# Scan of a Mamba block: the C product of five state indices on ScalarE in turned form, eight B products on GpSimd

## The reference

```python
x = silu(conv1d_depthwise(x, conv_w, 4 taps) + conv_b)           # 512 channels, 2048 steps
dt, Bm, Cm = split(x_proj_w @ x, [16, 32])                       # rank 16; 16 rows of B; 16 rows of C
dt = softplus(dt_w @ dt + dt_b)
A = -exp(A_log)                                                  # 512 x 16
def step(h, inp):
    h = exp(dt_t[..., None] * A) * h + (dt_t * u_t)[..., None] * B_t[:, None, :]
    return h, einsum('bdn,bn->bd', h, C_t)
y = ys + D * x
return y * silu(z)
```

## Time and profile before

| | |
|---|---|
| runs (us) | 8468.7, 8469.42, 8474.6; median 8469.42 |
| profiled execution | span 8471.3; no time beside the span is listed for it |
| scan phase in it | about 2600 to 6040 us after the span's start |
| busy over the span | TensorE 7608.0 (90%), VectorE 7340.3 (87%), ScalarE 5072.8 (60%), GpSimd 3704.5 (44%) |
| scans, L2022 | 2048, 1684.6 + 771.8 us busy |
| C products by GpSimd, L1707 | 1024, 2412.4 us busy |
| granted clock of TensorE, mean | 0.954 |

### The profile page before, as it was taken

One profiled execution on the slowest core, in us unless ns is written; L12 is line 12 of the kernel. 1 busy time (PEld: TensorE's weight loads), 2 busy tenths in 40 slices (PEclk: granted clock), 3 DMA queues, 4 the chain that ended last, 5 costly groups with the idle time before them and its releaser, 6 DMA issues. The chain is left out here.

```text
span 8471.3 us, 131822 instructions
## 1 busy us (share of the span) xinstructions
PE 7608.0 (90%) x38817; PEld 3068.7 (36%) x38818; DVE 7340.3 (87%) x10750; ACT 5072.8 (60%) x7665; POOL 3704.5 (44%) x1825
## 2 busy tenths in 40 slices
PE   6999999989987888888888888888889999999899
PEld 3333333325542333333333333333453333333355
DVE  6988888858877999999999999999658888888588
ACT  3577777762255666666665556556316777777622
POOL 0010011100016999999999999999400000110000
PEclk9899999989998999999999999999988999999999
DMA  6001101112262222222233333333561001010121
GB/s 177 18 19 20 19 19 19 20 37 70 67 232 91 85 83 83 84 83 83 83 98 103 100 100 100 101 103 97 164 181 18 19 19 19 19 22 18 36 78 61
DMA packets 531283, 603.88 MB, mean 71 GB/s; under 512 B 195488, under 2 KB 344736, under 8 KB 526560
## 3 DMA queue, kind: packets, MB, share of 16 engines
q1 hardware_dynamic: 526048, 562.63, 22.4%
q0 software_dynamic: 4608, 33.56, 2.0%
HBM read 397.75 MB, written 163.69 MB: 66 GB/s over the span
## 5 line engine op out<-in xcount | busy, mean ns | idle before, releaser
L833 DVE TENSOR_REDUCE ffn_att_mx<-psum 128x1 f32<-128x512 f32 (+3 forms) x4608 | 2728.0, 654 | 367.8 <-PE psum L674 209.2
L794 ACT ACTIVATE ffn_att_e<-psum,unscale 128x1024 f32<-128x1024 f32 (+3 forms) x2560 | 2376.5, 985 | 766.3 <-PE psum L739 760.3
L1707 POOL TENSOR_TENSOR scan_h<-scan_h,scan_cs 128x1024 f32<-128x1024 f32 x1024 | 2412.4, 2449 | 203.8 <-ACT scan_state L1878 198.0
L1788 PE MATMUL psum<-scan_h,ident 128*128 128x512 f32 x4096 | 1977.7, 624 | 158.9 <-POOL scan_h L1707 157.6
L2022 DVE TENSOR_TENSOR_SCAN scan_h<-psum,scan_state,scan_db 128x512 f32<-128x512 f32 x1408 | 1684.6, 1261 | 10.5 <-ACT psum L1920 10.5
L641 POOL TENSOR_SCALAR_AFFINE_SELECT ffn_att_e<-ffn_att_e 128x512 f32<-128x512 f32 x512 | 324.6, 634 | 3023.9 <-ACT ffn_att_e L794 3023.9
L674 PE MATMUL psum<-ffn_att_k,ffn_att_q 48*128 48x512 f16 (+3 forms) x5120 | 1438.8, 367 | 175.4 <-DMA ffn_att_v<-v 55.8
L1788 PEld LDWEIGHTS psum<-scan_h,ident 128*128 128x128 f32 x4096 | 777.7, 198 | 1321.1 <-issue 894.5
L705 PE MATMUL psum<-ffn_att_e,ffn_att_v 128*32 128x512 f32 (+3 forms) x10240 | 1240.4, 557 | 7.8 <-ACT ffn_att_o L809 2.4
L1920 ACT ACTIVATE psum<-scan_dt,scan_anr 128x512 f32<-128x512 f32 x1024 | 698.2, 682 | 460.2 <-DVE scan_h L2022 459.4
L674 PEld LDWEIGHTS psum<-ffn_att_k,ffn_att_q 48*128 48x128 f16 x5120 | 394.8, 94 | 1559.4 <-DVE ffn_att_mx L833 1260.7
(11 more groups left out here) (256 smaller groups left out, 7118.0 us busy)
## 6 DMA issues: line engine op xcount, KB each, us to landing
scan_cs<-scan_bcd SPq DMA_DIRECT2D x520, 256.0 KB, 3.2
scan_bs<-scan_bcd SPq DMA_DIRECT2D x162, 256.0 KB, 3.4
scan_win<-xp SPq DMA_DIRECT2D x34, 1036.0 KB, 7.0
scan_dt<-scan_sp POOLq DMA_DIRECT2D x32, 1024.0 KB, 7.0
mamba_out_ffn_in_ys<-yz SPq DMA_DIRECT2D x18, 1024.0 KB, 7.6
scan_yi<-y SPq DMA_DIRECT2D x17, 1024.0 KB, 6.7
ffn_att_q<-q_parts SPq DMA_DIRECT2D x128, 128.0 KB, 2.8
ao<-ffn_att_on SPq DMA_DIRECT2D x128, 128.0 KB
```

The lines of the kernel that those rows point to most:

```text
L794: nc.scalar.activation(E[:, s % PB, 2 * hp:2 * hp + 2, off:CH], psum[:, 2 * hp:2 * hp + 2, off:CH], ACT.Exp, scale=unscale[:, 0:1]).then_i ...
L833: nc.vector.reduce_max(mx[:, hh * 2 + pairs[0]:hh * 2 + pairs[1], i // HALF, i % HALF, c // TT], psum[:, turn, 0:(pairs[1] - pairs[0]) * w ...
L1707: nc.gpsimd.tensor_tensor(hh, hh, cs[:, n % NCS, :].unsqueeze(1).to_broadcast([P, 2, CH]), ALU.mult).then_inc(hc_ready, 1)
L1788: ins = nc.tensor.matmul(psum[:, m, :], ident[:, :], h[n % NH][:, m, :], start=False, stop=n == DS - 1)
```

## The change

Indices 5, 7, 9, 11, 13 (`TURN_N`) get another way to their C product. TensorE transposes h block by block (128 steps of all four tiles at a time, `turn_state`) into `BANK_X`, so that steps lie on partitions. There C_n is one number per partition: ScalarE's `times_c` copies the bank to SBUF with it as scale. TensorE transposes that back, adding into the sum (`turn_back`). C itself is turned once a chunk (`turn_c`, `keep_c`). The other eleven indices (`ROW_N`) keep GpSimd's product, now one instruction over four tiles, with one state copy for all four tiles. `POOL_N` grows from five to eight; `dbp` has two buffers and `db` one. TensorE sums an index two slots after its scan (`LAG`); `skip` and `read_y` move from slot 1 to 2; the convolution of a tile is one piece in slots 7, 9, 11, 13, and its copy follows in slots 8, 10, 12, 14. `dt_proj` of tiles 2 and 3 stands behind sums of its slot, and softplus_in comes in slots 3, 4, 4 and 5.

```diff
-    NH, NCS = 4, 8
-    POOL_N = (3, 6, 9, 12, 15)
+    NH, NT = 4, 4
+    TURN_N = (5, 7, 9, 11, 13)
+    ROW_N = [n for n in range(DS) if n not in TURN_N]
+    POOL_N = (1, 4, 6, 8, 10, 12, 14, 15)
+    POOL_AT = {14: 1, 1: 4, 3: 6, 5: 8, 7: 10, 9: 12, 11: 14, 13: 15}
+    DVE_AT = {n if (n - 1) % DS in DVE_N else (n - 1) % DS: n for n in DVE_N}
+    PE_X, PE_TURN_C, PE_SKIP, PE_Y, LAG = 0, 3, 2, DS - 1, 2
...
GpSimd
-                        for half in range(2):
-                            pool.wait_ge(carried, 2 * (DS * i + n) + half + 1)
-                            hh = h[n % NH][:, 2 * half:2 * half + 2, :]
-                            nc.gpsimd.tensor_tensor(hh, hh, cs[...].to_broadcast([P, 2, CH]), ALU.mult)
-                        if n + 3 in POOL_N:
-                            times_b(i, par, n + 3)
+                        if n in ROW_N:
+                            times_c(i, n)
                         if n == G_ADD:
                             softplus(i + 1, 1 - par)
+                        if n in POOL_AT:
+                            times_b(*chunk_of(i, par, 0 if POOL_AT[n] > n else DS)[:2], POOL_AT[n])
...
TensorE
+                def turn_state(i, n, tb):
+                    if tb:
+                        pe.wait_ge(hT_sb, turn_count(i, n, tb - 1))
+                    else:
+                        pe.wait_ge(scanned, UNITS * i + DM * (n + 1))
+                        ...
+                    for m in range(DM):
+                        ins = nc.tensor.transpose(psum[:, BANK_X, m * P:(m + 1) * P], h[n % NH][:, m, tb * P:(tb + 1) * P], ident[:, :])
+                    ins.then_inc(hT_ps, 1)
+                def turn_back(i, n, tb):
+                    pe.wait_ge(hT_sb, turn_count(i, n, tb))
+                    for m in range(DM):
+                        ins = nc.tensor.matmul(psum[:, m, tb * P:(tb + 1) * P], hT[tb % NT][:, m * P:(m + 1) * P], ident[:, :],
+                                               start=False, stop=False, is_transpose=True, skip_group_check=True)
+                    ins.then_inc(hT_summed, 1)
...
+                    for s in range(DS):
+                        n = s - LAG
+                        if s - 2 in TURN_N:
+                            turn_back(i, s - 2, TT - 1)
+                        if s == PE_X:
+                            x_proj(i + 1, 1 - par, way(1))
+                        if s == PE_TURN_C:
+                            turn_c(i + 1)
+                            dt_proj(i + 1, 0, way(1))
+                        if s == PE_TURN_C + 1:
+                            dt_proj(i + 1, 1, way(1))
+                        if s - 2 in TURN_N and TURN_N.index(s - 2) < DM:
+                            conv(i + 2, TURN_N.index(s - 2), way(2))
+                        if s - 1 in TURN_N:
+                            turn_state(i, s - 1, 0)
+                            if sums:
+                                sum_state(*here, (0, 1))
+                            turn_state(i, s - 1, 1)
+                            turn_back(i, s - 1, 0)
+                            if sums:
+                                sum_state(*here, (2,))
+                            turn_state(i, s - 1, 2)
+                            turn_back(i, s - 1, 1)
+                            if sums:
+                                sum_state(*here, (3,))
+                            turn_state(i, s - 1, 3)
+                            turn_back(i, s - 1, 2)
+                        elif s == PE_SKIP:
+                            for m in range(DM):
+                                skip(i, par, m, first, way(0))
+                                sum_state(*here, (m,))
+                        elif sums:
+                            sum_state(*here, (0, 1))
+                            if s == PE_TURN_C + 1:
+                                dt_proj(i + 1, 2, way(1))
+                            sum_state(*here, (2, 3))
+                        if s == PE_TURN_C + 2:
+                            dt_proj(i + 1, 3, way(1))
+                        if s in DVE_AT:
+                            next_row_b(...)
...
ScalarE
+                def times_c(i, par, n, tb, first):
+                    act.wait_ge(hT_ps, turn_count(i, n, tb))
+                    ...
+                    nc.scalar.activation(hT[tb % NT][:, :], psum[:, BANK_X, :], ACT.Copy, scale=cT[par][:, tb, DS + n:DS + n + 1]
+                                         ).then_inc(hT_sb, 1)
...
                         nc.scalar.activation(psum[:, BANK_A + k % 2, :], dt[par][:, m, :], ACT.Exp, ...).then_inc(decay, 1)
+                        if n - 1 in TURN_N and m >= 2:
+                            times_c(i, par, n - 1, m - 2, first)
+                        if n - 2 in TURN_N and m < 2:
+                            times_c(i, par, n - 2, m + 2, first)
...
+                        if (n, m) == (3, 2):
+                            softplus_in(i + 1, 1 - par, 0, way(1))
+                        if (n, m) == (4, 0):
+                            softplus_in(i + 1, 1 - par, 1, way(1))
+                        if (n, m) == (4, 2):
+                            softplus_in(i + 1, 1 - par, 2, way(1))
+                        if (n, m) == (5, 0):
+                            softplus_in(i + 1, 1 - par, 3, way(1))
...
+                        if m == 0 and n - 3 in TURN_N and TURN_N.index(n - 3) < DM:
+                            conv_out(i + 2, par, TURN_N.index(n - 3), way(2))
                         if (n, m) == (A_SILU, 1):
                             silu(i + 2, par)
```

More of the change, by code:

```diff
@@ L1721, in _, with taps @@
                 pe.wait_ge(diags, 2)
-                def taps(m, js, bank, rev):
-                    for j in js:
+                def taps(m, bank, rev):
+                    for j in range(TAPS):
                         off = 2 * HALO - j if rev else j
@@ L1829, in _ @@
                 in_steps(pe, step)
-                sum_state(M - 1, DS - 1)
+                for n in range(DS - LAG, DS):
+                    sum_state(M - 1, n, range(DM))
             @block.scalar
@@ L1873, in softplus_ln, with carry @@
                     nc.scalar.activation(sp1[:, m, :], sp1[:, m, :], ACT.Ln, bias=1.0).then_inc(logs, 1)
-                def carry(n, half, ends, rev):
-                    ms = slice(2 * half, 2 * half + 2)
-                    kept = zeros[:, ms] if ends else h[n % NH][:, ms, LAST[rev]]
-                    nc.scalar.activation(state[:, n, ms], kept, ACT.Copy).then_inc(carried, 1)
+                def carry(n, ends, rev):
+                    kept = zeros[:, :] if ends else h[n % NH][:, :, LAST[rev]]
+                    nc.scalar.activation(state[:, n, :], kept, ACT.Copy).then_inc(carried, 1)
+                def times_c(i, par, n, tb, first):
+                    act.wait_ge(hT_ps, turn_count(i, n, tb))
+                    if not (first and n == TURN_N[0]):
+                        act.wait_ge(hT_summed, turn_count(i, n, tb) - NT)
+                    nc.scalar.activation(hT[tb % NT][:, :], psum[:, BANK_X, :], ACT.Copy, scale=cT[par][:, tb, DS + n:DS + n + 1]
+                                         ).then_inc(hT_sb, 1)
                 def read_y(i, m):
@@ L1894, in _ @@
                 middle(0, 0)
+                keep_c(0, 0)
                 for m in range(DM):
@@ L2023, in step @@
                                                      state[:, n, m:m + 1], ALU.mult, ALU.add).then_inc(scanned, 1)
-                        if n == 1 and not first and way(-1):
+                        if n == PE_SKIP and not first and way(-1):
                             read_y(i - 1, m)
```

266 lines of the change are left out of this document (145 added, 121 removed).

## The result

After the change the kernel takes **8734.4 us** (median of 4 runs, 8728.1 to 8747.9); before, beside it, 8469.1 (8465.5 to 8474.6). The ratio is 1.0318, 95% interval 1.0305 to 1.0332: slower by 265 us, where 86 had been forecast. The profiled execution has a span of 8726.3 us, 255 more than before.

The account below looks back on a forecast made before the run. VectorE and GpSimd were both full; afterwards order, not a full engine, decides. Forward chunks +4.1 us, reverse +1.1, chunk end +3: 16 x 4.1 + 16 x 1.1 + 3 = +86 on 8471.3, so 8555 us; own range 8470 to 8640.

Parts of the forecast that it names:

- Direction and kind: Whole scan phase: slower, no engine full, order decides; VectorE's decay waits rise from 73 to some 400 us.
- A turned index, 1.0 us: Slots of indices 5, 7, 9, 11: TensorE's cycle of 1.73 us against a 1.175 us scan loses 1.0 us each.
- Index 13 and the SiLU, 4.35 us: Slots 14 and 15: late convolution copy loses 1.2 us, last product ahead of the SiLU 3.15; together 4.35 per chunk.
- Slots 2 to 5: VectorE waits for a decay behind softplus_in and dt_proj of tile 3: 4.4 us lost forward, 2.5 in reverse.
- the low clock: TensorE at 1.2 GHz before dt_proj: half of 1.65 us, 0.8, counted in forward chunks.
- the lower bound of the prediction: Slot 5 with no queue in GpSimd: decay 11.4 us after the scans of index 3 against 8.2, losing 3.2.
- the 4.4: Loss in us in slot 5, forward: GpSimd's back-to-back queue brings the decay at 25.9, VectorE wants it at 21.5.
- "The rest of the program isn't touched": Everything outside the scan phase, 5.0 ms, was taken as unchanged.
- Rival (b), the clock falls in the turned stretches: TensorE at low clock in turned slots: 9130 us, or 8820 with one fall per index; chance 0.15.

Follow-up runs that it names:

- e14: Changed kernel with scaled copies of turned indices (not 13) half a slot earlier on ScalarE, one row sum in each gap between TensorE's turns: 8718.7 us.
- e18: e16 with the row sums of tiles 2 and 3 of the index before a turned one moved behind the next slot's convolution: 8433.2 us.
- e3: Changed kernel with the row sums of tiles 2 and 3 in turned slots moved behind all four turns of the state on TensorE: 8732.3 us.
- e10: Changed kernel with all turned indices' scaled copies half a slot earlier on ScalarE, two row sums in each gap between TensorE's turns: 8914.8 us.
- e2: Changed kernel with softplus_in(1) one unit later on ScalarE, so the state copy and a decay stand ahead of it: 8667.2 us.
- e4: Changed kernel with the last scaled copy of index 13 moved from ahead of the SiLU to behind the decay of (15,2): 8655.7 us.
- e6: Changed kernel with ten extra row matmuls that compute nothing, put into TensorE's idle stretch ahead of the skips: 8708.8 us.
- e7: Changed kernel with the next chunk's delta steps (split, turn of C, delta matmuls, softplus_in) moved earlier on VectorE, TensorE and ScalarE: 8598.8 us.
- e11: e7 with softplus_in back at the changed kernel's places and the row matmul of slot 3 inside the sum of index 1: 8570.7 us.
- e13: Changed kernel with 115 instructions that only wait, added to VectorE's scan part so later phases lie where they did before the change: 8695.4 us.
- e16: Changed kernel with the orders of e11 and e14, the index 13 copy moved as in e4, and the 115 instructions of e13: 8445.3 us.

## Why the prediction was wrong, step by step

- **Direction and kind: right.** No engine is full, VectorE's waits for the decay went from 73 to 456 us (about 400 said), GpSimd is busy 91 and 92 us a chunk (94 said), idle ahead of C products for 731 us, the B products are 257 of 2.288 us.
- **A turned index, 1.0 us: right in size**, two waits of VectorE of 0.55 and 0.28 us, 1.03 us in all between the starts of the scans (said: 0.55 and 0.45). e14 and e18 support the cause named, TensorE's order in the cycle; e3 and e10 show that moving the sums in it is not enough. VectorE in a turned stretch of after:

```profile
5382.51 1.28 DVE L2147 TENSOR_TENSOR_SCAN scan_h<-psum,scan_state,scan_db 128x512 f32<-128x512 f32 x1 [0.55 <-ACT psum L2022]
5384.07 2.46 DVE L2147 TENSOR_TENSOR_SCAN scan_h<-psum,scan_state,scan_db 128x512 f32<-128x512 f32 x2 [0.28 <-ACT psum L2022]
```

- **Index 13 and the SiLU, 4.35 us: right** (1.4 + 3.3 in slots 14 and 15).
- **Slots 2 to 5: the step that failed.** It said "GpSimd starts C(1) ..., then B(4), C(2), C(3)" back to back, 19.5 us, with 4.4 + 0.8 us lost forward and 2.5 in reverse. Lost were 7.0 and 7.5: 16 x 1.8 + 16 x 5.0 = 109 us of the 139 by which the scans missed. Two things were left out. The state copy of index 3, which releases C(3), stands on ScalarE behind softplus_in(1), and that waits for dt_proj(1) (e2: 67 us). In the reverse chunk shown, C(3) starts 3.2 us after the scans of index 3, and the scan that waits for the decay 14.5 us after them, where the lower bound of the prediction has 11.4; GpSimd's queue, by which the 4.4 was worked out, stands idle there. And the low clock was counted as half a fall in forward chunks and none in reverse. The size of a fall was about right (1.65 said, 1.6 measured), but it comes in 12 of the 15 forward chunks behind the first, and in reverse, where the reads of y keep TensorE idle for mostly 5.4 us ahead of the skips, in all 16: the reverse chunk has the worse case, not the milder (e4, e6). The turn of C and its copy ahead of dt_proj(0), for which ScalarE waits 4.1 us in the reverse chunk shown, have no term in the sum; slot 3 lost 1.0 and 1.9 us. e7 and e11 removed 4 to 5 us of the 7 by order alone.
- The other 30 us of the scans' miss are about 1 us a chunk, in tenths over several slots (slot 6, the first turned index); they were not taken apart.
- **"The rest of the program isn't touched": wrong by 32 us.** Its code is the same, but not the place of its loops in VectorE's program (e13, e16). With the place of before the last phase and attention 2 are as long as before again.
- **Rival (b), the clock falls in the turned stretches: no.** In one of the changed kernel, 5379.5 to 5392.0, the granted clock is 1.00, four transposes start to end in 0.60 us (windows of after):

```profile
5379.50:5392.00 12.50, 10.83 (x47) 5.81 (x46) 11.16 (x9) 10.33 (x19) 9.05 (x2) 1.00 0.40 126
```

The exception is the start of index 5, behind the wait of slot 5: its first turn takes 1.11 us in all 32 chunks and the second over 0.9 in 12; the other 18 turns of a chunk take 0.60 to 0.66 (timeline of after, TensorE):

```profile
5373.29 1.11 PE L1844 MATMUL psum<-ident,scan_h 128*128 128x128 f32 x4 [5.78 <-DVE scan_h L2147]
```

By the rule of the Trainium skill (TensorE: Matmul & The Clock Gate, Part 4) that transposes do not bring the full clock, 0.27 us each would have held; here four take 0.60 among matmuls, and the trace disagrees. A long run of transposes alone is in no trace here.

## What to carry to other kernels

A cost estimate that adds up each queue by itself isn't enough where a small operation of one engine (here a state copy of 0.2 us) releases a long one of another: list for each such release what stands ahead of it in its own queue, and what that waits for. When work is moved between engines and the time rises with all of them idle, try orders before giving the division up: here the same work went from 8734 to 8445 us by order and placement. Judge an edit by the change of each slot, not by the total: e3, e10 and e18 each shortened the slots that they were meant to shorten and paid for it in others.
